# Set-up: third key group masked earlier, values 0 to 3 made in another bank; the ends of attention and the border reordered

## Chip, cores and metric

The kernel runs on one core of a Trainium2 chip. The metric is the device time in microseconds (us), the median of three runs. Engines are named as in the profile: PE (TensorE, matmul), DVE (VectorE), ACT (ScalarE), POOL (GpSimd), SP (the queue that issues plain DMAs). Each engine takes its instructions strictly in the order of the program and waits on semaphores.

## The reference, cut to what matters

There are 16 sequences of 128 tokens with 128 features (x), and a context of 77 rows of 64 features for each. Two layers run one after the other:

```
x = x + tanh(g_xattn[l]) * cross_attention(layernorm(x), ctx)   # 16 heads of 8, softmax over the 77 rows
x = x + tanh(g_ffn[l])   * moe(layernorm(x))                    # 8 experts of 128 -> 512 -> 128, top 2 per token
```

Layer 0's experts use the tanh form of GELU, without biases; its combination weights are the two top softmax probabilities, normalised to sum 1. Layer 1 has biases everywhere, ReLU experts, and its moe is `layer_norm(t + sum of the two experts) * gamma + beta`, with t the normalised x. All is float32.

## The kernel before

**Set-up.** Weights and context are turned on PE. Keys and values of layer 0 come from `keys` (PE), masked to a block form by `masked` (ACT or DVE), and `vals` (PE), masked by `values_kept` (DVE, counted by the semaphore `v_kept`). Group g of the keys holds six batches; group 2 lies in bank 7 of the eight PSUM banks. Values of batches 0 to 3 (`VE` = 4) are made at once in bank 2, batches 4 to 15 one at each step of attention (`late_batch`, `more_values`). `upper_scores` of batch 0 waits for `v_kept` to reach 4. `unread` issues n matmuls of 512 columns whose result nobody reads.

**Attention** is a software pipeline, written out by hand, of steps s = 0 to 17 (`B` = 16) and a `tail`, and each engine has its own `step(s)`. In step s, batch s is normalised and turned, batch s-1 gets its q, batch s-2 its scores (first pass: `scores_for_max`, from which DVE's `maxima` takes each head's maximum; second pass: `scores`, from which `less_max` subtracts it; then four Exp on ACT), and batch s-3 the weighted values, the division and `residual`. Banks 2 and 3 hold the upper first scores.

**Routing** works on pairs of batches, named by the odd one. `row_stats` (DVE), `deviations` (POOL), a normalisation into `xfa` (POOL; by DVE for the last pair), `turn_rows` (PE), `copied` (ACT), `logits` (PE), `read_logits` and `choose` (DVE: top two), `ranks` (PE: how many earlier tokens went to each expert), `counted` (POOL: running count), `read_ranks` and `place` (DVE: row numbers), `scatter` (POOL: an indirect DMA per batch and choice, into the row buffer `xg_rows`). `chosen(s)` and `placed(s)` say which pair is chosen and which is placed in step s: s-6 and s-7 where these are odd. The last pairs are LAST = 15, PRIOR = 13, THIRD = 11; THIRD is ranked and placed in the tail.

**Route.** When all is counted, `route` (DVE) computes for 39 tiles of 128 rows the expert `t_e`, the first row `r_row`, which rows are valid and where results go; `tiles0`/`tiles1` tell the others. `gate_gaps` and `gate_weights` make the two combination weights. SP (`load_tiles`) waits for the flag and for all scatters, then loads tiles into four buffers.

**Experts.** In step s of the tile loop PE turns tile s, does the first stage of tile s-1 and the second of tile s-2; ACT copies the turned tile and applies the activation; DVE copies the expert's w1 for tile s (`w1s`, two buffers), computes the destination rows `ids` of tile s-1 and copies the result of tile s-2 out; POOL scatters the result into `o_rows`. SP reloads a buffer when its `ids` are computed.

**Border.** After layer 0's loop PE makes the values of layer 1's batches 0 to 7, DVE runs `late` (biases and gains of layer 1) and masks these values, SP gathers the results, and DVE adds them to x (`stats_of`) and takes the statistics of layer 1's first batches.

## Time and profile before

| what | value |
|---|---|
| median of 3 runs | 464.51 us (464.02 to 465.03) |
| profiled execution: its own time | 464.98 us |
| its span | 463.2 us, 15660 instructions |
| PE matmul busy | 382.5 us, 83% |
| DVE busy | 328.4 us, 71% |
| POOL busy | 232.8 us, 50% |
| ACT busy | 214.1 us, 46% |
| attention, layer 0, with set-up | 0 to about 115 us |
| expert tiles, layer 0 | about 134 to 213 us |
| attention, layer 1 | about 227 to 327 us |
| expert tiles, layer 1 | about 346 to 424 us |

The rows further down come from this one profiled execution; their times count from the start of its span. A busy share is an average over stages with different limits, so it does not say by itself which engine sets a stage. TensorE's granted clock has two levels here, 1.2 and 2.4 GHz.

### The profile page before, as it was taken

The numbers are of one execution on the slowest core, as the hardware profiler recorded it, in microseconds if no ns is written. First come the engines' busy times: TensorE is split into PE (matmuls) and PEld (weight loads), VectorE is DVE, ScalarE is ACT, GpSimd is POOL, SyncE is SP. The second block draws the span as 40 slices with busy tenths as digits, with TensorE's granted clock in tenths as the row PEclk, the third lists the DMA queues.
The fourth block names the chain that finished last, engine by engine and source line by source line (L and its number), as shares of the span: only waits on it lengthen the run. The fifth ranks groups of instructions, "written<-read, shape, count | busy, mean of one in ns | idle before, by whom it ended". The sixth has DMA issues, their size and how long they took to land.

```text
span 463.2 us, 15660 instructions
## 1 busy us (share of the span) xinstructions
PE 382.5 (83%) x5357; PEld 306.1 (66%) x5357; DVE 328.4 (71%) x1164; ACT 214.1 (46%) x607; POOL 232.8 (50%) x370
## 2 busy tenths in 40 slices
PE   8699999997839999999899988998739999997000
PEld 4466666665539999996356666666729999997000
DVE  4558899987765666667558989987654666666592
ACT  3534555544514444441255555553525666665022
POOL 7313367768713544453203357767742445455176
PEclk9879999999559999998979999999888999999555
DMA  6969000011112222221201010001211223221612
GB/s 174 331 143 297 5 16 27 28 34 38 52 48 56 72 72 73 72 66 51 71 18 33 26 36 28 27 28 54 68 55 44 72 66 77 71 77 43 186 36 57
DMA packets 38690, 32.73 MB, mean 71 GB/s; under 512 B 6984, under 2 KB 32245, under 8 KB 38613
## 3 DMA queue, kind: packets, MB, share of 16 engines
q1 hardware_dynamic: 34069, 22.12, 18.0%
q0 software_dynamic: 4544, 9.61, 6.6%
q8 instruction: 45, 0.74, 0.7%
q14 instruction: 32, 0.26, 0.2%
HBM read 20.50 MB, written 11.21 MB: 68 GB/s over the span
## 4 chain that ended last, share of the span: by engine, by line
PE 57%; DVE 17%; issue 9%; POOL 9%; DMA 5%; ACT 1%; SPq 1%; DVEq 0%; POOLq 0%; ACTq 0%
PE banks L693 52%; PE banks L696 5%; DVE mx L1337 4%; POOL xg_rows L575 4%; DMA room<-xg_rows 2%; DVE room L1404 2%; DVE x L1321 1%; POOL wa L670 1%; DMA xg_rows<-xfa,slots 1%; DVE mxp L1346 1%; DVE wa L1635 1%; DMA o_rows<-room,ids 1%; DVE fstats L1422 1%; DVE wa L1628 1%; ACT room L1103 1%
## 5 line engine op out<-in xcount | busy, mean ns | idle before, releaser
L648 POOL DMA_INDIRECT o_rows<-room,ids x78 | 76.4, 980 | 96.4 <-DVE room L1572 44.6
L693 PE MATMUL banks<-room 128*128 128x128 f32 x624 | 86.0, 282 | 0.8 <-ACT room L1196 0.2
L693 PE MATMUL banks<-wa,room 128*128 x624 | 82.9, 276 | 0.5 <-ACT room L1191 0.4
L693 PEld LDWEIGHTS banks<-room 128*128 128x128 f32 x624 | 78.6, 198 | 2.7 <-issue 2.6
L693 PEld LDWEIGHTS banks<-wa,room 128*128 128x128 f32 x624 | 76.1, 192 | 0.9 <-issue 0.8
L575 POOL DMA_INDIRECT xg_rows<-xfa,slots x64 | 64.2, 1003 | 20.1 <-issue 18.8
L1103 ACT ACTIVATE room<-banks 128x384 f32<-128x384 f32 x128 | 52.4, 496 | 28.2 <-PE banks L693 28.2
L1337 DVE TENSOR_REDUCE mx<-banks 128x8 f32<-128x648 f32 x64 | 50.2, 825 | 12.2 <-PE banks L693 11.9
L1196 ACT ACTIVATE room<-banks,b_cols 128x128 f32<-128x128 f32 x156 | 44.6, 368 | 26.5 <-PE banks L693 26.1
L1058 ACT ACTIVATE room<-banks 128x128 f32<-128x128 f32 (+1 forms) x110 | 31.2, 283 | 49.0 <-PE banks L696 49.0
L1549 DVE COPY room<-wa 128x512 f32 x78 | 33.3, 427 | 28.7 <-issue 21.4
L1404 DVE RECIPROCAL room<-banks 128x128 f32<-128x128 f32 x32 | 30.5, 953 | 7.4 <-PE banks L693 7.2
L1191 ACT ACTIVATE room<-banks 128x512 f32<-128x512 f32 x39 | 23.3, 598 | 26.1 <-PE banks L693 26.1
L693 PE MATMUL banks<-kz,room 32*128 32x324 f32 x256 | 32.8, 499 | 3.0 <-issue 2.2
L696 PE MATMUL banks<-ident,room 128*128 128x128 f32 x78 | 22.5, 288 | 15.4 <-DMA room<-xg_rows 14.9
L693 PE MATMUL banks<-room,kz 32*128 32x128 f32 x768 | 32.8, 301 | 0.4 <-issue 0.4
L693 PE MATMUL banks<-room,keep 128*32 128x128 f32 x768 | 28.8, 285 | 2.3 <-ACT room L1103 2.3
L693 PEld LDWEIGHTS banks<-room,v_s 128*32 128x32 f32 x768 | 20.1, 113 | 15.1 <-ACT room L1103 14.6
L693 PE MATMUL banks<-room,v_s 128*32 128x128 f32 x768 | 28.8, 285 | 0.3 <-DVE x L1413 0.2
L693 PEld LDWEIGHTS banks<-room,kz 32*128 32x128 f32 x768 | 26.4, 198 | 2.8 <-issue 0.5
L565 POOL TENSOR_SCALAR rstd<-mv 128x2 f32<-128x2 f32 x16 | 3.8, 239 | 45.9 <-DVE mv L1307 42.1
L693 PE MATMUL banks<-wide 128*128 128x512 bf16 x85 | 24.7, 452 | 1.4 <-POOLq L286 1.4
(188 smaller groups left out, 656.3 us busy)
## 6 DMA issues: line engine op xcount, KB each, us to landing
room<-xg_rows SPq DMA_DIRECT2D x78, 68.5 KB, 1.9
wa<-in_L_ffn_w SPq DMA_DIRECT2D x1, 2048.0 KB, 10.4
wb<-in_L_ffn_W SPq DMA_DIRECT2D x1, 2048.0 KB, 16.7
ob<-o_rows SPq DMA_DIRECT2D x32, 64.0 KB, 2.0
wb<-o_rows SPq DMA_DIRECT2D x6, 256.0 KB, 4.8
o_rows<-room,ids POOLq DMA_INDIRECT x78
x<-in_x SPq DMA_DIRECT2D x4, 256.0 KB, 4.4
xg_rows<-xfa,slots POOLq DMA_INDIRECT x64
```

The source lines that it names most:

```text
L575: pool.indirect_dma_start(out=xg_dram, in_=xfa[:, at, :], in_offset=None, out_offset=bass.IndirectOffsetOnAxis(ap=slots[:, at, k:k + 1], a ...
L648: pool.indirect_dma_start(out=o_dram[l], in_=o_sb[t.slot(UN)][:, :], in_offset=None, out_offset=bass.IndirectOffsetOnAxis(ap=ids[t.slot(UN ...
L670: pool.tensor_tensor(nrm[:, b, :], nrm[:, b, :], gam[:, :], ALU.mult).then_inc(l_gam, 1)
L693: return pe.matmul(out_, lhsT, rhs, start=start, stop=stop)
L696: return pe.transpose(out_, in_, idn[0:n, 0:n])
L1058: return act.activation(out_, in_, ACT.Copy)
L1103: act.activation(probs[b.slot(2)][g][:, :], bank[(4, 5, 0, 1)[g]][0:M, 0:NC * T], ACT.Exp)\
L1191: act.activation(hid[:, :], bk[:, :], func).then_inc(S["act"].sem, FC)
L1196: act.activation(hid[:, c * P:(c + 1) * P], bk[:, c * P:(c + 1) * P], func, bias=b1_cols[:, bass.ds(e4 + c, 1)]).then_inc(S["act"].sem, 1)
L1337: dve.tensor_reduce(mx[r][:, G * g:G * (g + 2)].rearrange("p (i j) -> p i j", i=2), two.rearrange("p i (j k) -> p i j k", j=G), AX.X, ALU. ...
L1404: dve.reciprocal(den[:, :], bank[6][:, T:2 * T]).then_inc(rc.sem, 1)
L1549: dve.tensor_copy(w1s[s.slot(2)][:, :], wa1[:, bass.ds(e, F)]).then_inc(S["wc"].sem, 1)
```

## The change

- Set-up: DVE masks key group 2 (bank 7) in step 1 and no longer in step 2. `vals` of batches 0 to 3 go to bank 7 in step 2, behind the first scores of batch 0, and their masking follows batch 0's `maxima`. The first scores no longer wait for `v_kept`. Two filler matmuls of four go.
- Ends of attention, both layers: pair THIRD is chosen in step 16 and ranked and placed in step 17, not in the tail; POOL's scatters of pairs 7, 9 (FOURTH) and 11 are put in another order; pair PRIOR is normalised by DVE (`normalised`), not POOL.
- `route`: the tile rows come from sums of differences instead of a selection by expert, and a new flag `rowsT` is told as soon as they are there; SP's tile loads wait for it instead of `tiles`.
- Masked values of layer 1: batches 8 to 11 behind the route; batches 12 to 15 at steps 2 to 5 of layer 0's tile loop on DVE. `gate_weights` moves to step 6 of both loops, `late` to step 8 of layer 0's, the scaled weights `w01g` to its step 10.
- ACT runs a one-column Gelu ahead of layer 0's tiles and a one-column Exp behind them (`preload`).
- Filler matmuls: 34 and 18 instead of 12 behind the attention of layers 0 and 1; 30 instead of 42 at the border.

The diff, without the declarations of tiles and flags:

```diff
@@ -239,6 +238,9 @@
...
         altbase = sb("altbase", [P, NT])
+        region7 = sb("region7", [P, E])
+        first_row = sb("first_row", [P, NT])
+        preload = sb("preload", [P, 2])
@@ -369,12 +371,17 @@
...
         def chosen(s):
+            if s.c >= B:
+                return THIRD if s.c == B else None
...
         def placed(s):
+            if s.c > B:
+                return THIRD
...
-        LAST, PRIOR, THIRD = Step(B - 1), Step(B - 3), Step(B - 5)
+        LAST, PRIOR, THIRD, FOURTH = Step(B - 1), Step(B - 3), Step(B - 5), Step(B - 7)
@@ -445,7 +452,7 @@
...
                 S = layers[l]
-                hear(sp, f"tiles{l}")
+                hear(sp, f"rowsT{l}")
@@ -555,6 +562,9 @@
...
                 iota(altbase[:, :], [[P, NT]], NPAIR, 1)
+                iota(first_row[:, :], [[P, NT]], P, 0)
+                link(pool.memset(region7[:, :], float(REGION)))
+                link(pool.memset(region7[:, E - 1:E], 0.0))
@@ -599,10 +609,16 @@
...
                         deviations(b4)
+                    if live_pair(b4) and b4.c < B - 3:
...
                                                frs[:, j, 1:2], ALU.subtract, ALU.mult).then_inc(S["f2"].sem, 1)
+                    if s.c == B:
+                        placed_rows(FOURTH.back(2))
+                        scatter(FOURTH.back(2), 1)
+                    if s.c == B + 1:
+                        scatter(FOURTH, 1)
@@ -617,21 +633,22 @@
...
                         counted(placed(s))
-                    for b, js in ((b8, (0, 1) if s.c == B + 1 else (0,)), (b9, (1,))):
-                        if live_pair(b):
+                    for b, js in ((b8, (0,)), (b9, (1,))):
+                        if live_pair(b) and s.c < B:
...
                                 scatter(b, j)
+                    if s.c == B:
+                        placed_rows(FOURTH)
+                        scatter(FOURTH, 0)
+                    if s.c == B + 1:
+                        placed_rows(THIRD)
+                        scatter(THIRD, 0)
                 def tail():
-                    counted(THIRD)
-                    placed_rows(THIRD)
-                    scatter(THIRD, 0, (0,))
+                    scatter(THIRD, 1)
                     deviations(LAST)
-                    scatter(THIRD, 0, (1,))
-                    scatter(THIRD, 1, (0,))
                     counted(PRIOR)
-                    scatter(THIRD, 1, (1,))
@@ -716,7 +733,7 @@
...
-                return ("kza0_0", "kzd0_0") if (l, g) == (0, 0) else ("kzd0_2",) if (l, g) == (0, 2) else (f"kza{l}_{g}",)
+                return ("kza0_0", "kzd0_0") if (l, g) == (0, 0) else () if (l, g) == (0, 2) else (f"kza{l}_{g}",)
@@ -749,10 +766,7 @@
...
                     if s == 0:
-                        unread(bank[2][:, :], 4)
-                    if s == 1:
-                        for b in range(VE):
-                            vals(0, b, bank[2][:, b * NC * G * HD:])
+                        unread(bank[2][:, :], 2)
@@ -788,7 +802,6 @@
...
                         hear(pe, "woS")
-                        pe.wait_ge(v_kept, VE)
@@ -911,6 +922,10 @@
...
                         lower_scores(b2)
+                    if l == 0 and s.c == 2:
+                        hear(pe, "kzd0_2")
+                        for b in range(VE):
+                            vals(0, b, bank[7][:, b * NC * G * HD:])
@@ -921,6 +936,8 @@
...
                         ranks(placed(s), s)
+                    if s.c == B:
+                        logits(THIRD, bank[7])
@@ -930,7 +947,7 @@
...
                         project(b3)
-                    if live_pair(b5):
+                    if live_pair(b5) and s.c < B:
@@ -943,6 +960,8 @@
...
                             S["f3"].wait(pe, chosen(s), 1)
+                        if placed(s):
+                            S["f4"].wait(pe, placed(s), 1)
@@ -951,7 +970,6 @@
...
                     values(LAST, bank[5])
-                    ranks(THIRD, Step(B + 2))
@@ -1035,7 +1053,7 @@
...
                 tail()
-                unread(bank[2 if l == 0 else 4][:, :], 12)
+                unread(bank[2 if l == 0 else 4][:, :], 34 if l == 0 else 18)
@@ -1047,7 +1065,7 @@
...
                     S["oc"].wait(pe, Step(NT - 1))
-                    unread(bank[0][:, :], 42)
+                    unread(bank[0][:, :], 30)
@@ -1170,6 +1188,8 @@
...
                     say(act.activation(gexp[:, :], gap[:, :], ACT.Exp), f"gexp{l}")
+                    if l == 0:
+                        act.activation(preload[:, 0:1], zero_row[:, 0:1], ACT.Gelu_apprx_tanh)
@@ -1208,6 +1228,8 @@
...
                 pipeline(act, NT, 8, 1, experts(l))
+                if l == 0:
+                    act.activation(preload[:, 1:2], zero_row[:, 0:1], ACT.Exp)
@@ -1267,12 +1289,8 @@
...
                         hear(dve, "keep")
-                    if s == 2:
+                    if s == 1:
                         masked(2, range(G), bank[7])
-                    if s == 1:
-                        dve.wait_ge(v_made, VE)
-                        for b in range(VE):
-                            values_kept(b, bank[2][:, b * NC * G * HD:])
@@ -1431,6 +1449,8 @@
...
                         maxima(b2)
+                    if l == 0 and s.c == 2:
+                        kept_from(range(VE), bank[7], 0)
@@ -1438,6 +1458,10 @@
...
                         read_ranks(placed(s))
+                        if s.c > B:
+                            place(placed(s))
+                    if s.c == B + 1:
+                        normalised(PRIOR)
@@ -1453,24 +1477,26 @@
...
                         row_stats(b3)
-                    if placed(s):
+                    if placed(s) and s.c <= B:
...
+                def normalised(b):
+                    S["rs2"].wait(dve, b)
+                    for j in range(2):
+                        dve.tensor_scalar(xfa[:, b.c - 1 + j, 0:D], x[:, seq(b.back(1 - j))], fmv[:, j, 0:1],
+                                          frs[:, j, 1:2], ALU.subtract, ALU.mult).then_inc(S["f2"].sem, 1)
...
                     S["lg"].wait(dve, PRIOR)
-                    read_ranks(THIRD)
                     read_logits(PRIOR, bank[7])
-                    place(THIRD)
...
                     choose(PRIOR)
-                    S["rs2"].wait(dve, LAST)
-                    for j in range(2):
-                        dve.tensor_scalar(xfa[:, LAST.c - 1 + j, 0:D], x[:, seq(LAST.back(1 - j))], fmv[:, j, 0:1],
-                                          frs[:, j, 1:2], ALU.subtract, ALU.mult).then_inc(S["f2"].sem, 1)
+                    normalised(LAST)
@@ -1493,26 +1519,24 @@
...
                 total(cE[:, :], cmp8[:, :, :])
-                link(tt(fE[:, :], cE[:, :], tE[:, :], ALU.subtract))
+                link(dve.scalar_tensor_tensor(dA[:, :], tE[:, :], float(-P), region7[:, :], ALU.mult, ALU.add))
+                link(tt(dB[:, :], region7[:, :], nE[:, :], ALU.subtract))
+                link(tt(dB[:, 0:E - 1], dB[:, 0:E - 1], nE[:, 1:E], ALU.add))
                 link(tt(t8a[:, :, :], inner(iotat[:, :], E), bc3(cE[:, :], NT), ALU.is_ge))
+                link(tt(t8b[:, :, :], t8a[:, :, :], bc3(dA[:, :], NT), ALU.mult))
+                total(t_up[:, :], t8b[:, :, :])
+                link(tt(t8b[:, :, :], t8a[:, :, :], bc3(dB[:, :], NT), ALU.mult))
+                total(t_end[:, :], t8b[:, :, :])
+                link(tt(t_up[:, :], t_up[:, :], first_row[:, :], ALU.add))
+                link(dve.scalar_tensor_tensor(t_row[:, :], t_end[:, :], nE[:, 0:1], t_up[:, :], ALU.add, ALU.min))
+                link(dve.tensor_copy(r_row[:, :], t_row[:, :]))
+                tell(dve, f"rowsT{l}")
                 total(t_e[:, :], t8a[:, :, :])
-                link(tt(t8a[:, :, :], bc3(iota8[:, :], NT), inner(t_e[:, :], E), ALU.is_equal))
-                link(tt(t8b[:, :, :], t8a[:, :, :], bc3(nE[:, :], NT), ALU.mult))
-                total(t_n[:, :], t8b[:, :, :])
-                link(tt(t8b[:, :, :], t8a[:, :, :], bc3(fE[:, :], NT), ALU.mult))
-                total(t_f[:, :], t8b[:, :, :])
-                link(tt(t_j[:, :], iotat[:, :], t_f[:, :], ALU.subtract))
-                link(ts(t_j[:, :], t_j[:, :], float(P), None, ALU.mult))
-                link(ts(t_n[:, :], t_n[:, :], float(-P), None, ALU.add))
-                link(tt(t_rel[:, :], t_j[:, :], t_n[:, :], ALU.min))
                 link(ts(t_ec[:, :], t_e[:, :], float(E - 1), None, ALU.min))
-                link(dve.scalar_tensor_tensor(t_row[:, :], t_ec[:, :], float(REGION), t_rel[:, :], ALU.mult, ALU.add))
-                link(ts(r_row[:, :], t_row[:, :], float(P), None, ALU.add))
...
-                link(dve.scalar_tensor_tensor(t_valid[:, :], t_rel[:, :], iotap[:, :], t_j[:, :], ALU.add, ALU.is_ge))
+                link(dve.scalar_tensor_tensor(t_valid[:, :], t_row[:, :], iotap[:, :], t_up[:, :], ALU.add, ALU.is_ge))
@@ -1574,25 +1598,29 @@
...
                         ins.then_inc(S["oc"].sem, 1)
+                    if l == 0 and 2 <= s.c < 6:
+                        kept_from((s.c + 10,), bank[7][:, (s.c - 2) * NC * G * HD:], B + 4 + s.c - 2)
+                    if s.c == 6:
+                        gate_weights(l)
+                    if l == 0 and s.c == 8:
+                        dve.wait_ge(ld["w1"], 16 * len(LATE))
+                        late()
+                    if l == 0 and s.c == 10:
+                        link(dve.tensor_scalar(w01g[:, :], w01[:, :], tg[:, 2:3], None, ALU.mult))
...
                 link(dve.memset(cum[:, :], 0.0))
-                if l == 1:
-                    link(dve.tensor_scalar(w01g[:, :], w01[:, :], tg[:, 2:3], None, ALU.mult))
...
                 tail()
-                if l == 0:
-                    kept_from(range(8, 12), bank[5], B)
...
                 if l == 0:
-                    kept_from(range(12, B), bank[7], B + 4)
-                gate_weights(l)
+                    kept_from(range(8, 12), bank[5], B)
@@ -1600,8 +1628,6 @@
...
                 if l == 0:
-                    dve.wait_ge(ld["w1"], 16 * len(LATE))
-                    late()
...
                 else:
```

## Rows read from the trace of the kernel before

**Rows 1.** The page, clock in 40 slices; chain that ended last, by engine.

```profile
PEclk9879999999559999998979999999888999999555
...
PE 57%; DVE 17%; issue 9%; POOL 9%; DMA 5%; ACT 1%; SPq 1%; DVEq 0%; POOLq 0%; ACTq 0%
```

**Rows 2.** Timeline of set-up: start, length, engine, line, tile [idle before, its end].

```profile
13.85 3.13 ACT L1066 ACTIVATE kz<-banks,zero_row,mask 128x486 f32<-128x486 f32 x4
...
14.71 1.95 DVE L1243 TENSOR_TENSOR v_s<-banks,keep_v 128x384 f32<-128x384 f32 x4 [2.79 <-PE banks L693]
...
16.88 0.83 PE L693 MATMUL banks<-kz,room 32*128 32x324 f32 x8 [2.23 <-issue]
...
17.74 1.57 DVE L1337 TENSOR_REDUCE mx<-banks 128x8 f32<-128x648 f32 x2 [1.07 <-PE banks L693]
...
20.00 1.67 PE L693 MATMUL banks<-room,kz 32*128 32x128 f32 x24
...
20.16 2.29 DVE L1238 TENSOR_SCALAR kz<-banks,mask 128x324 f32<-128x324 f32 x4
```

**Rows 3.** Timeline of the end of attention, layer 0.

```profile
112.97 0.20 DVE L1367 MAX8 top<-lg 128x8 f32<-128x8 f32 x2
...
113.85 0.18 DVE L1379 TENSOR_TENSOR mb<-oh 128x16 bf16<-128x16 f32 x1
...
115.35 0.60 DVE L1472 TENSOR_SCALAR xfa<-x,fmv,frs 128x128 f32<-128x128 f32 x2 [1.32 <-POOL frs L567]
...
119.86 0.96 POOL L575 DMA_INDIRECT xg_rows<-xfa,slots  x1 [0.30 <-issue]
```

**Rows 4.** Timeline of the route, layer 0: a wide step, the tile rows.

```profile
125.19 0.48 DVE L1500 TENSOR_TENSOR room<-iota,t_e 128x312 f32<-128x312 f32 x1
...
129.34 0.33 DVE L1512 TENSOR_SCALAR r_row<-t_row 128x39 int32<-128x39 f32 x1
```

**Rows 5.** Timeline of the first tiles, layer 0.

```profile
133.99 0.45 PE L696 MATMUL banks<-ident,room 128*128 128x128 f32 x1 [7.57 <-DMA room<-xg_rows]
...
137.53 1.28 ACT L1191 ACT_TABLE_LOAD   x1 [1.86 <-PE banks L693]
...
139.55 1.15 PE L693 MATMUL banks<-wa,room 128*128 x8 [0.40 <-ACT room L1191]
```

**Rows 6.** Timeline of a steady tile, layer 0.

```profile
143.23 0.43 DVE L1549 COPY room<-wa 128x512 f32 x1 [0.30 <-issue]
...
144.44 1.06 PE L693 MATMUL banks<-room 128*128 128x128 f32 x8
144.53 0.29 DVE L1572 COPY room<-banks 128x128 f32<-128x128 f32 x1 [0.25 <-PE banks L693]
...
145.12 0.43 DVE L1549 COPY room<-wa 128x512 f32 x1 [0.29 <-issue]
```

**Rows 7.** Timeline of the border between the layers.

```profile
213.33 0.20 DVE L1287 CAST bo<-bo_in 1x128 bf16<-1x128 f32 x1
...
216.62 10.92 PE L693 MATMUL banks<-wide 128*128 128x512 bf16 x42
216.65 3.81 DVE L1243 TENSOR_TENSOR v_s<-banks,keep_v 128x384 f32<-128x384 f32 x8
...
220.80 0.74 DVE L1321 SCALAR_TENSOR_TENSOR x<-ob,w01g,x 128x128 f32<-128x128 f32 x2
...
225.65 0.49 ACT L1111 ACTIVATE xn<-x,rstd 128x128 f32<-128x128 f32 x1 [13.85 <-POOL rstd L617]
...
227.38 0.27 PE L696 MATMUL banks<-ident,xn 128*128 128x128 f32 x1
...
232.46 1.28 ACT L1103 ACT_TABLE_LOAD   x1
```

**Rows 8.** Timeline of the first tiles, layer 1.

```profile
346.18 0.45 PE L696 MATMUL banks<-ident,room 128*128 128x128 f32 x1 [6.51 <-DMA room<-xg_rows]
...
350.95 1.17 PE L693 MATMUL banks<-wa,room 128*128 x8
```

More of the change, by code:

```diff
@@ L191, in build @@
         cE = sb("cE", [P, E])
-        fE = sb("fE", [P, E])
+        dA = sb("dA", [P, E])
+        dB = sb("dB", [P, E])
         t8a = part("experts", P, NT * E).rearrange("p (t e) -> p t e", t=NT)
@@ L195, in build @@
         t_e = sb("t_e", [P, NT])
-        t_n = sb("t_n", [P, NT])
-        t_f = sb("t_f", [P, NT])
-        t_j = sb("t_j", [P, NT])
-        t_rel = sb("t_rel", [P, NT])
+        t_up = sb("t_up", [P, NT])
+        t_end = sb("t_end", [P, NT])
         t_valid = sb("t_valid", [P, NT])
@@ L281, in build @@
                     f"{k}{l}_{g}" for l in range(2) for k, n in (("k", 3), ("kzd", 3), ("kza", 3))
-                    for g in range(n)) + tuple(f"{k}{l}" for l in range(2) for k in ("count", "tiles", "gap", "gexp"))}
+                    for g in range(n)) + tuple(f"{k}{l}" for l in range(2) for k in ("count", "rowsT", "tiles", "gap", "gexp"))}
         def tell(eng, name):
@@ L849, in more_values @@
                     if late_batch(s.c) is not None:
-                        if late_batch(s.c) == VE:
-                            hear(pe, "kzd0_2")
                         pe.wait_ge(v_kept, late_batch(s.c))
```

## The prediction

> **What bounds it now.** I read the page first. The chain that ended last is 57% TensorE and 17% VectorE [rows 1], and no engine sets the whole: attention alternates between PE and DVE, the expert tiles are paced by PE, and at four seams (set-up, the end of each attention, the border between the layers) PE waits for others. The clock line shows the same seams: full speed is 9, and slices 1 and 2 (from 11.6 to 34.7 us), 10 and 11 (115.8 to 139.0), and some around the border and the start of layer 1's tiles are lower [rows 1]. Then I read the timeline at each seam.
>
> In set-up the first scores start at 16.88, after PE idled 2.23 us; just before, DVE finished the masked values of batches 0 to 3 at 14.71 + 1.95 = 16.66, the count that the scores wait for [rows 2]. At the end of attention POOL issues scatters at 0.96 + 0.30 = 1.26 us each; eight (pairs 13 and 15) run without a gap from 119.86, so the last ends at 119.86 + 7 x 1.26 + 0.96 = 129.64 [rows 3], and the first tile reaches PE at 133.99, awaited by DMA [rows 5]. A steady tile takes 145.12 - 143.23 = 1.89 us, and DVE idles only 0.25 in it [rows 6]. At the border layer 1's first transpose, at 227.38, stands behind 42 filler matmuls that take 10.92 us; its input was ready at 225.65 + 0.49 = 226.14 [rows 7].
>
> **1. Set-up.** Removed: the wait for the values ahead of the first scores. Q is scaled on ACT just before ACT starts its masking at 13.85 [rows 2], so the scores can start near 14.0, not 16.88. DVE's masking of key group 2 (2.29 us [rows 2]) moves into the gap of 2.79 us ahead of the values [rows 2]: from about 11.95 to 14.25. It hides behind the wait for the first scores; were it later than 14.85, maxima would be late by the difference. First maxima: scores 14.0 + 0.86 (17.74 - 16.88) = about 14.85, against 17.74: 2.9 earlier. What is late next is ACT: the second score pass also needs batch 1's q, which ACT gives only behind its masking, at 13.85 + 3.13 = 16.98 [rows 2], so that pass starts near 17.6 and not 20.00, 2.4 earlier. The values' 1.95 us of DVE now follow the first maxima, and end near 18.8 (14.85 + 1.57 + 0.4 for two small ones + 1.95), before the second scores exist near 20. POOL's iota and two memsets add under 1 us to a queue whose next result, the third batch's statistics, is not late. The second price is the clock: two slices at 8 and 7 tenths [rows 1] mean 11.58 x (0.4 + 0.6) = 11.6 us at half speed. If it stays as it is, I take 3.0; if PE, with fewer gaps, kept 2.4 GHz, half of the 5.8 us that PE-bound work would lose comes back as well, to 5.9. I take 4.0, nearer the first end, because PE still has holes while it waits for maxima and q.
>
> **2. Ends of attention, both layers.** Pair 11 is now chosen, ranked and placed a step sooner, and pair 7's second scatter goes ahead of POOL's wait for ranks: both fill idle POOL time. Against it, in step 16 PE's logits (about 0.5) stand before the transpose of the maxima, and DVE's choice (112.97 to 114.03, 1.06 [rows 3]) before batch 15's maxima: the last batch is 1.5 us later. POOL no longer normalises pair 13, but its deviations of pair 15 now stand behind both scatters of pair 11 and one more half of pair 9. Counted from place(9) at about 104.6 in that order (six scatters at 1.26 through pair 11, two deviations at 1.1, count 0.5, issue gaps of 0.3 to 0.5), they end at 117.8, against 115.35 [rows 3]; DVE waits in order for them, then places pair 13 at 118.95, and pair 13's scatters start at 119.25, not 119.86: **-0.6 per layer** (bounds -1.5, if all POOL idle closed, and +0.9). Queued behind DVE's wait are pair 13's slots and pair 15's logits; pair 15's placing comes 2.45 later.
>
> The route: its tile rows ended at 129.34 + 0.33 = 129.67. Values 8 to 11 (1.95 by rows 2) leave the stretch before it; two wide steps of 0.51 (0.48 and a gap) and a few small ones go, 1.6 together; place(15) adds 2.45. So the new flag comes at 129.67 - 1.95 - 1.6 + 2.45 = 128.6, ahead of the scatters' landing: the sooner flag is worth nothing here, and the cover is about 2 us [rows 3, 4].
>
> **3. First tiles.** In layer 0 PE went from the first transpose (133.99) to the first second-stage matmul (139.55) in 5.56 us, at half clock and with a table load of 1.28 [rows 1, 5]. 34 fillers instead of 12 start near 124.8: some 7 at 0.43 and 27 at 0.21 (slow and fast form of the same matmul: 10.92/42 = 0.26 is their mix [rows 7]) end near 133.5, when the first tile arrives at 133.4. At full clock the transpose halves, the two first-stage groups take about 1.0 each (1.06 in rows 6) and the table is there: 3.2 us. So 5.56 - 3.2 + 0.6 = **-2.9** (only -1.0 if the clock is down; fillers that run over cost up to +1). In layer 1: 350.95 - 346.18 = 4.77 [rows 8] becomes 3.4 if six more fillers hold the clock: with the 0.6, **-2.0** (clock down: -0.6).
>
> The row gives the load 1.28, with the Gelu ready to follow at its end [rows 5]. The Trainium skill (ScalarE: Activation LUTs, "What ACT_TABLE_LOAD costs") adds a drain of about 1.38 us, 2.66 for a switch; by it the border below would win 1.4 more and the sum would be 9.8 instead of 8.4. The row decides against it.
>
> **4. DVE work moved into layer 0's loop.** Four value batches at steps 2 to 5 (1.95/4 = 0.49, single 0.55: 2.2), the gate weights at step 6 (three small ones, 0.75 with their gaps), the late biases at step 8 (213.33 to 216.65, 3.3 [rows 7]): 6.2 us, where DVE idles 0.25 a tile and the copy of w1 is ready at 143.66 for a matmul at about 144.35, 0.7 of slack [rows 6]. Over steps 2 to 8: 6.2 - 7 x 0.25 - 0.7 = 3.8 of PE standing still, 2.7 of it after step 8. PE is the pace, so it is lost: **+3.8** (bounds 0, if the work fits gaps that the start leaves, and 6.2). The loads of later tiles wait for DVE's ids, 3.3 later too, but PE is late by nearly as much. The scaled weights at step 10 are one small instruction, inside a tile's 0.25. In layer 1 the gate weights alone meet 0.7 + 0.25 of slack: 0 to 0.1.
>
> **5. Border.** DVE's queue ahead of the first combination at 220.80 loses the 3.3, but waits for the values (v 0 to 3 near 214.4, 4 to 7 near 216.7) and the gathered rows, which land near 219.3: 1.5 sooner. That makes the first normalised batch ready at 226.14 - 1.5 = 224.6. Twelve fillers fewer (0.21 to 0.26 each) free PE at 227.38 - 2.55 = 224.8. So the transpose is **-2.5** (bounds 1.5 and 3.1). The Exp table's 1.28 at 232.46 [rows 7] stood behind a wait that ends 0.45 later: **-0.8** (to -1.28).
>
> **Sum.** -4.0 - 2.9 + 3.8 - 2.5 - 0.8 - 2.0 = -8.4. The profiled execution took 464.98 (span 463.2 and 1.78 around it): 456.6; the runs' median is 0.47 below it: **456.1 us**, 1.8% faster. 0.2%, 0.9 us, is about what a measurement of this kernel tells from no change.
>
> **Rivals.**
> - *Half clock.* Fillers and holes don't hold 2.4 GHz: set-up -3.0, layer 0's tiles -1.0, layer 1's -0.6, the rest the same: -3.0 - 1.0 + 3.8 - 3.3 - 0.6 = -4.1, 460.4. For it: the clock was low at every one of these seams [rows 1]. Against: the fillers now reach to the first tile. 0.18.
> - *DVE's pieces are hidden in the loop* (the first tiles leave it slack): -12.2, 452.3. Against: 0.25 idle a tile [rows 6]. 0.10.
> - *The order at the end of attention costs.* DVE waits for POOL's deviations behind scatters; if the last scatters end 1.9 later and not 0.6 sooner, twice: -8.4 + 5.0 = -3.4, 461.1. For it: DVE already sat 1.32 for them [rows 3]. Against: the eight scatters were the bound, and DVE's wait must pass 2 us to displace them. 0.10.
> - *Slower: PE's clock falls after the standstill at step 8.* At 1.2 GHz a tile is PE-bound at 3.8, so each tile loses 1.9; it decides from (8.4 + 0.9)/1.9 = 4.9 tiles, some 19 us at half clock. For ten tiles: -8.4 + 19 = 475. For it: a tile's transpose and w1 copy resume after 2.7 us of silence. Against: the dips at the seams are one or two slices long [rows 1]. 0.05.
> - *It does nothing:* the seams close, but each gain is paid back at the next wait, as with the 3.8. Within 0.9 of 464.5. 0.05.
>
> **Chances and range.** My forecast, with the clock of set-up either way (454.2 to 457.6), has 0.52; the rivals share the other 0.48. From 452 to 461.3 it leaves out the slower case, no change, and tails: 0.15 to 0.2. Faster by over 0.2%: 0.90; within 0.05; slower 0.05.
>
> **What would show it.** First maxima near 14.9 and second near 20.2; slices 1 and 2 of the clock line; first scatter of pair 13 near 119.3 on its own count, less the set-up's gain; first tile to second-stage matmul 3.2 us with no table load; PE's idle before the first-stage matmuls of tile 9 about 2.7 us, waiting for the w1 copy; first transpose of layer 1 2.5 us nearer to the last tile. Wrong if the late biases stall nothing, if the fillers run past the first tile, or if the scatters' end moves later.

## The result, and the profile after

The changed kernel took 461.0 us, median of five runs (459.81 to 462.1), the kernel before 464.44 beside it: ratio 0.9936, 95% interval 0.9915 to 0.9956. It is 3.4 us faster; 8.4 were forecast. The profiled execution took 461.97, its span is 460.1, 3.1 less than before, and that is where the stages below are read.

The page, clock in 40 slices, which answers to [rows 1]:

```profile
PEclk9589999999599899999769999999899999999555
```

Slice 1 is now at 5 tenths and the border (slices 19 and 20) at 7 and 6, where before it was 9 and 9. Timelines of the changed kernel (start, length, engine, line, tile, idle before and what ended it); set-up, against [rows 2]:

```profile
13.88 1.46 PE L710 MATMUL banks<-kz,room 32*128 32x324 f32 x8
...
15.40 1.57 DVE L1355 TENSOR_REDUCE mx<-banks 128x8 f32<-128x648 f32 x2 [1.47 <-PE banks L710]
```

The scores start at 13.88, as forecast, but run at half clock (1.46, not 0.83), so first maxima came at 15.40, not 14.9. Batch 14's maxima moved from 98.74 to 95.69: 3.05. (In the three quiet profiles with the old set-up they come at 97.60 to 98.74, in the six with the new one at 93.86 to 95.87, so the means are 3.1 apart; "quiet" is explained below.)

End of attention and first tiles, against [rows 3 to 5]:

```profile
115.84 1.06 POOL L585 DMA_INDIRECT xg_rows<-xfa,slots  x1 [1.00 <-DVE slots L1415]
...
121.48 9.08 PE L710 MATMUL banks<-wide 128*128 128x512 bf16 x33 [0.33 <-issue]
...
124.95 0.18 DVE L1533 CAST r_row<-t_row 128x39 int32<-128x39 f32 x1
...
130.40 0.27 PE L713 MATMUL banks<-ident,room 128*128 128x128 f32 x1
...
133.59 1.15 PE L710 MATMUL banks<-wa,room 128*128 x8
```

From batch 14's maxima to the first tile it takes 34.71 instead of 35.25, and from there to the first second-stage matmul 3.19 instead of 5.56: 2.9 in all, as forecast. Step 8 of layer 0's loop, where `late` stands, against [rows 6]:

```profile
146.79 0.20 DVE L1305 CAST bo<-bo_in 1x128 bf16<-1x128 f32 x1
...
150.52 0.43 DVE L1573 COPY room<-wa 128x512 f32 x1 [0.70 <-DVE bet L1317]
...
151.09 1.13 PE L710 MATMUL banks<-room 128*128 128x128 f32 x8 [2.01 <-DVE room L1573]
...
152.06 1.59 PE L710 MATMUL banks<-wa,room 128*128 x8
```

PE stands still for 2.01 us, waiting for w1's copy, and then its matmuls take 1.59 where they took 1.06: the granted clock is at 0.50 for 3.4 us, from 152.4. In stretches:

```profile
146.00:150.00 4.00, 2.77 (x23) 2.38 (x22) 3.39 (x15) 1.48 (x4) 1.93 (x2) 1.00 0.27 72
150.00:154.00 4.00, 2.91 (x19) 2.94 (x20) 2.56 (x11) 0.70 (x2) 0.96 (x1) 0.80 0.07 20
154.00:158.00 4.00, 4.00 (x30) 4.00 (x29) 2.09 (x9) 1.32 (x4) 1.21 (x2) 0.77 0.26 68
```

(Stretch; then its length, busy us of PE, weight loads, DVE, ACT and POOL with their counts; then the granted clock, the DMA share and GB/s.) The border, against [rows 7]:

```profile
213.76 6.42 PE L710 MATMUL banks<-wide 128*128 128x512 bf16 x29 [0.16 <-issue]
223.41 0.33 PE L713 MATMUL banks<-ident,xn 128*128 128x128 f32 x1 [3.23 <-ACT xn L1129]
...
225.36 1.46 PE L710 MATMUL banks<-kz,room 32*128 32x324 f32 x8 [0.24 <-ACT room L1148]
```

```profile
218.02 0.74 DVE L1339 SCALAR_TENSOR_TENSOR x<-ob,w01g,x 128x128 f32<-128x128 f32 x2 [1.71 <-DMA ob<-o_rows]
```

In the kernel before PE had 10.92 us of fillers here and came late; now they end at 220.2, PE idles 3.23, and the scores run at half clock. DVE idles 1.71 for the gathered rows. The first tiles of layer 1, against [rows 8]:

```profile
342.77 0.30 PE L713 MATMUL banks<-ident,room 128*128 128x128 f32 x1 [2.30 <-DMA room<-xg_rows]
343.61 0.45 PE L713 MATMUL banks<-ident,room 128*128 128x128 f32 x1 [0.54 <-ACT room L1076]
344.10 2.05 PE L710 MATMUL banks<-room 128*128 128x128 f32 x8
```

The fillers end 2.30 before the tile, and the first group takes 2.05, half clock again.

In some sets of runs the kernel before took 463 to 466 us (below: quiet), in others 493 to 496, where PE idled in attention with nothing to wait for (below: starved; the last section shows it), and there the ratios say little of the edits but the stages outside attention can still be read.

### The profile page after: what moved, and what is told of

The parts are those of the page before. It is cut to its first block, busy times and chain, and to the rows that moved or that the text cites. A ratio compares the mean times of both kernels' runs of the same rounds, so it can differ in the third digit from the quotient of the medians.

```text
span 460.1 us, 15686 instructions
## 1 busy us (share of the span) xinstructions
PE 387.5 (84%) x5368; PEld 308.5 (67%) x5371; DVE 326.1 (71%) x1164; ACT 214.7 (47%) x609; POOL 229.6 (50%) x369
## 4 chain that ended last, share of the span: by engine, by line
PE 50%; DVE 17%; POOL 14%; issue 11%; DMA 5%; ACT 1%; DVEq 0%; ACTq 0%; SPq 0%; POOLq 0%
PE banks L710 46%; POOL xg_rows L585 7%; PE banks L713 4%; DVE mx L1355 4%; DMA o_rows<-room,ids 3%; DVE room L1422 2%; DVE x L1339 2%; POOL wa L687 1%; POOL frs L577 1%; DVE mxp L1364 1%; DVE stats L1322 1%; DVE wa L1661 1%; DVE wa L1654 1%; POOL xfa L615 1%; DVE lst L1664 1%
## 5 line engine op out<-in xcount | busy, mean ns | idle before, releaser
L710 PE MATMUL banks<-kz,room 32*128 32x324 f32 x256 | 34.7, 525 | 0.4 <-ACT room L1148 0.2
L710 PE MATMUL banks<-wide 128*128 128x512 bf16 x96 | 25.9, 429 | 2.0 <-POOLq L288 1.4
```

Of the source, the lines that this page charges most:

```text
L710: return pe.matmul(out_, lhsT, rhs, start=start, stop=stop)
```

## The experiments

Stages are differences between two events of one profile, so they don't hold what happened ahead of them: *loop* is first second-stage matmul to last result copy of layer 0, *border* the last copy to layer 1's first maxima, *start* layer 1's first to third batch's maxima, *tile 1* first transpose to first second-stage matmul.

**42 fillers at the border** (quiet)

```diff
-                    unread(bank[0][:, :], 30)
+                    unread(bank[0][:, :], 42)
```

> The changed kernel (461.0 us) with 42 filler matmuls at the border again instead of 30. Theory 1, the clock: 30 fillers at full clock end at 220.2 and PE stands still for 3.2 us before layer 1's first transpose at 223.41, and the granted clock falls at 223.5. Twelve more at 0.21 fill 2.5 of the 3.2; the clock stays at 2.4 GHz through 226, the first transpose stays near 223.4, first maxima of layer 1 come 1.0 sooner (2.5 behind the transpose as before the change, not 3.5), and the following steps gain 0.5 to 1.5 more: 1.5 to 2.5 us in all, 458.5 to 459.5. Theory 2, the gathered rows bound the border and the clock falls anyway because PE has holes there: the first transpose and the first maxima stay where they are, 460.8 to 461.2. A third outcome: the fillers run over the transpose, 461.5.

459.84, ratio 0.9873 (0.9837 to 0.9908). Beside the version of layer 1's fillers below, which is the same up to layer 1's tiles, the border took 15.14 instead of 16.03 and the stretch to batch 14's maxima 80.84 instead of 81.49: 1.5 won, at the low end of theory 1. From the last copy to batch 14's maxima it takes 96.0 and 95.8 in the two quiet profiles with 42 fillers and `late` off the border, 97.4 and 97.5 in the two with 30. The scores of the first batch took 0.83; but the clock fell all the same, at 228.15, which is 6.7 us behind the first transpose and not 0.7, and stayed down for 6.8 us and not 13.7:

```profile
220.00:224.00 4.00, 3.76 (x24) 1.82 (x22) 0.58 (x4) 1.68 (x5) 1.31 (x5) 1.00 0.29 83
224.00:228.00 4.00, 2.31 (x36) 1.38 (x35) 2.92 (x8) 1.77 (x5) 0.17 (x1) 1.00 0.06 17
228.00:232.00 4.00, 4.00 (x40) 2.25 (x42) 2.01 (x4) 1.23 (x5) 0.00 (x0) 0.52 0.06 16
```

(Columns as above.) PE is busy 2.31 of 4 us ahead of the fall: it waits 1.69 for the first maxima.

**`late` behind the loop again** (quiet)

```diff
-                    if l == 0 and s.c == 8:
-                        dve.wait_ge(ld["w1"], 16 * len(LATE))
-                        late()
...
+                    dve.wait_ge(ld["w1"], 16 * len(LATE))
+                    late()
                     kept_from(range(4), bank[3], B + 8)
```

> The changed kernel with the late biases and gains (late) back behind layer 0's tile loop on DVE, where they were, and all else kept. Theory A, the loop pays for late twice, in PE's wait of 2.0 for the w1 copy and in a clock that falls behind it: the last result copy of layer 0, at 211.00, comes 4.4 sooner (2.7 stall, 1.7 clock) near 206.6, and at the border late takes DVE for 3.3 while the gathered rows land, of which 1.7 was idle anyway, so 0.5 to 1.5 comes back: 457 to 458. Theory B, the prediction's own sum: only the 2.7 of the stall comes back, and the border loses 1.6 to 3.3: 460 to 461.5. If the clock still falls near 150 without late, it is the value batches or the early tiles that make it fall.

455.87, ratio 0.9787 (0.9752 to 0.9823): the lowest ratio of all. The loop took 74.38, beside 77.56 with `late` in it in the same set of runs: 3.2 back. At `late`'s own place more came back: from the seventh to the eleventh result copy it takes 7.98 here, 11.99 to 12.00 in all five profiles with `late` in step 8, and 7.6 to 7.9 in the five others that have the rest of the work in the loop and not `late` in step 8. So `late` cost 4.0 to 4.4, theory A; the clock fell behind it in all five (3.4 us at 0.50, 1.7 us of work) and in none of the six. The rest of the difference lies in single tiles that come 0.3 to 0.6 late, others in each profile. The border paid 0.5 (16.53 for 16.03). These stages explain some 3 us; the ratio lies 7 us under the changed kernel's 0.9936, which was not run again in this set, so the ratio is not all this edit's.

The value batches were still in steps 2 to 5, and cost nothing: the first five result copies are 7.7 us apart in this version and the changed one, 8.0 before. DVE took them between a result copy and w1's next copy without a gap:

```profile
137.75 0.29 DVE L1596 COPY room<-banks 128x128 f32<-128x128 f32 x1 [0.18 <-PE banks L710]
137.96 0.55 DVE L1265 TENSOR_TENSOR v_s<-banks,keep_v 128x384 f32<-128x384 f32 x1
138.42 0.42 DVE L1573 COPY room<-wa 128x512 f32 x1
```

In [rows 6] that copy has 0.30 of idle ahead of it, put down to issue. With a piece before it that idle is gone, so DVE's room in a tile was 0.25 + 0.30, not 0.25. The gate weights at step 6 did cost: the next two result copies take 4.1 us and not 3.8, in every version with them there.

**28 fillers behind layer 1's attention** (quiet)

```diff
-                unread(bank[2 if l == 0 else 4][:, :], 34 if l == 0 else 18)
+                unread(bank[2 if l == 0 else 4][:, :], 34 if l == 0 else 28)
```

> The changed kernel with 28 instead of 18 filler matmuls behind layer 1's attention. PE idled 2.3 us between the last filler (340.47) and the first tile (342.77), and the clock fell at 343.8. Theory 1, the clock: ten more at 0.21 take 2.1 and close that hole; the first tile's transpose stays near 342.8, and the first second-stage matmul follows in 3.4 instead of 4.67: 1.3 sooner, 459.7. Theory 2, holes between the tile's first steps let the clock fall whatever stands ahead of them: no change, 461.0. If the fillers run over the first tile: up to 0.5 slower.

459.73, ratio 0.9839 (0.9799 to 0.9879). Tile 1 took 3.61 instead of 4.67, and PE idled 0.41 ahead of it, not 2.30: 1.1 won, theory 1 (in the two other quiet versions with 18 fillers it took 4.53 and 5.23, in the other with 28 it took 3.58). The rest of the ratio is not this edit's.

**The set-up alone, on the kernel before** (quiet): the hunks of steps 0 to 2, `kept` and the wait for `v_kept`.

> The kernel before with only the change of the set-up: key group 2 masked in step 1, values 0 to 3 in bank 7 behind the first scores, two fillers of four. If the set-up gives its gain by itself: first maxima near 15.4 instead of 17.74, batch 14's maxima 3.0 sooner, 464.4 - 3.0 = 461.4, and the clock falls near 12 as in the changed kernel; then all other parts together (of which the prediction wanted -4.4) are worth only about -0.4. If part of these 3.0 comes from the new order in the last steps: 1.5 to 2.5 less than before, 462 to 463.

461.31, ratio 0.9915 (0.9878 to 0.9951), as much as the whole change. So all the other parts together gave about nothing in the changed kernel, within the some 2 us that the intervals leave; the table of stages below says the same.

**Four more fillers in set-up**, behind `woT` (starved; set-up lies ahead of where that bites)

```diff
                 say(tr(bank[3][:, 0:P], w_nat[:, 1, :], P), "woT")
+                unread(bank[1][:, :], 4)
```

> The changed kernel with four more fillers in set-up, where PE waited 1.2 us (10.82 to 12.03) for the first normalised batch. Theory 1, the clock of set-up falls for want of work there: with the hole closed it stays at 2.4 GHz to 28 us and batch 14's maxima come 1.0 to 1.5 sooner: 460 to 460.5. Theory 2: it falls by chance or for the holes behind (runs of the same set-up showed it fall at 12, at 19, or not at all): no change, 461.0.

502.34, ratio 1.0179 (1.0118 to 1.0241). They closed the hole (0.17 of idle instead of 1.21 ahead of the first transpose), and the clock fell at 17.9; in seven profiles with the new set-up and without these fillers it fell at 17.1 to 18.2:

```profile
16.00:20.00 4.00, 2.72 (x32) 1.88 (x34) 2.67 (x9) 2.54 (x8) 0.48 (x2) 0.74 1.06 298
20.00:24.00 4.00, 4.00 (x42) 2.32 (x44) 1.92 (x4) 1.23 (x6) 0.00 (x0) 0.50 0.94 252
```

Its fourth batch's maxima came at 33.2, as with `late` behind the loop (33.16). In three of the eleven other profiles of the changed set-up, all without these fillers, the clock did not fall in the first 40 us; in one of them, that of the 42 fillers at the border, those maxima came at 30.7 and batch 14's at 93.86, 4.9 sooner than before the change. So theory 1, the hole, fell, by this one profile. What decides between the two stays open; it is 1 to 2 us from one execution to the next. The Trainium skill (TensorE: Matmul & The Clock Gate, "Part 1: The HAM clock gate") says that the number of matmuls at the low clock at a kernel's start varies from run to run. What varies here is another thing, a fall from 12 us on, after the clock was up; no run here shows the start itself vary.

**The order at the ends of attention alone**, on the kernel before: all hunks of `chosen`, `placed`, steps 16 and 17 and the tails.

> The kernel before with only the new order at the ends of both attentions (pair 11 chosen, ranked and placed sooner, pair 13 normalised by DVE, POOL's scatters in the new order). The prediction gave it -0.6 per layer. From batch 14's maxima to the first tile the kernel before took 35.25 and 34.89, the changed one 34.71 and 34.41, so 0.5 per layer: 464.4 - 1.0 = 463.4. Rival: batch 15's later maxima (1.3 us) cost as much as POOL gains, and the 0.5 came from the route's sooner flag or from chance: 35.2 and 34.9 again, 464.2 to 464.8.

Starved: 502.12, ratio 1.0183 (1.0129 to 1.0236); repeated, still starved, 502.02, 1.0156 (1.0107 to 1.0204). Once more, quiet:

> The same kernel as e10_order_only. Where the kernel before takes 464: 463.4 if the new order is worth 0.5 per layer, 464.2 to 464.8 if batch 15's later maxima eat it. Where PE is short of instructions: 1.015 to 1.02, as twice before.

464.14, ratio 1.0035 (1.0009 to 1.006): no gain, rather a loss. The last scatter ended 23.75 behind the last maxima instead of 25.64 (of which 1.3 is only that the last maxima are later), but the first tile came 6.06 behind it instead of 4.31. The old flag, told behind `t_alt`, was the last; the scatters had ended at 127.94:

```profile
131.01 0.20 DVE L1538 TENSOR_TENSOR t_alt<-altbase,t_alt 128x39 f32<-128x39 f32 x1
```

```profile
132.04 2.82 SPq L466 DMA_DIRECT2D room<-xg_rows  x4
```

SP left 0.83 behind the end of this instruction. In the kernel before SP left 1.35 behind it, and 2.32 behind the end of the last scatter:

```profile
128.72 0.96 POOL L575 DMA_INDIRECT xg_rows<-xfa,slots  x1 [0.30 <-issue]
130.45 0.20 DVE L1517 TENSOR_TENSOR t_alt<-altbase,t_alt 128x39 f32<-128x39 f32 x1
132.00 7.53 SPq L461 DMA_DIRECT2D room<-xg_rows  x6
```

So the old flag had only some 0.5 us to spare there. So the order was tried together with the route's new arithmetic and flag:

> The kernel before with the new order at the ends of attention and with the route's new arithmetic and its sooner flag for the tile loads, nothing else. With the order alone the last scatter ended 23.7 behind the last maxima instead of 25.6, but the first tile came 6.06 behind it instead of 4.3, for the old flag was told at 131.2 and the load left at 132.0. Theory A, the flag is what the order needs: the first tile comes 4.3 behind the last scatter and 28.0 behind the last maxima (order alone 29.8, before 29.95), and the time is 1 to 2 us under the order alone, ratio 0.996 to 1.000. Theory B, the prediction's, that the sooner flag is worth nothing: as the order alone, 1.0035. For layer 1 the order alone already had 4.43 behind the scatter, so nothing changes there by either.

Starved: 500.32, ratio 1.0172 (1.0132 to 1.0212). But the first tile came 5.19 behind the last scatter, where the order alone in starved runs had 7.27 and 7.29: the flag, with the arithmetic that makes it sooner, is worth 2.1 there, theory A in kind, though not down to its 4.3. In a quiet run this pair was not measured.

**First tiles of layer 0 alone**, on the kernel before: 34 fillers and the one-column Gelu.

> The kernel before with only two edits at the first tiles of layer 0: 34 fillers instead of 12 and the one-column Gelu ahead of the tiles. The prediction's 5.56 to 3.2: first transpose to first second-stage matmul takes 3.2, 464.4 - 2.4 = 462.0. Rival: the sooner start is given back in the loop, where the first tiles then wait for DVE: 464. A second look at the same edit: without DVE's pieces in the loop, the stretch from first second-stage matmul to last copy should stay at 73.6 as in the kernel before, not 77.4.

Starved: 498.05, ratio 1.0062 (1.0022 to 1.0102); repeated, 495.76, 1.0043 (1.0009 to 1.0078). Tile 1 took 3.19 both times and the loop 73.59 and 73.27: nothing is given back in it. But the fillers ran over the tile, which came 10.0 behind the last scatter. The Gelu without more fillers, quiet:

```diff
+                    if l == 0:
+                        act.activation(preload[:, 0:1], zero_row[:, 0:1], ACT.Gelu_apprx_tanh)
```

> The kernel before with the one-column Gelu ahead of layer 0's tiles, and its 12 fillers kept. It splits the 5.56 to 3.19 between first transpose and first second-stage matmul: the table load took 1.28, so 4.3 if that is all that it costs, and the clock's share is 1.1; by the Trainium skill (ScalarE: Activation LUTs, what a table load costs) up to 2.66 would go with the load, and then 2.9 to 3.2 remain and the fillers are worth next to nothing here. In time: 463.2 or 462.1 where the kernel before takes 464.4. Where PE is short of instructions, the first tile comes 7 behind the last scatter and not 10, since 12 fillers don't reach it.

463.16, ratio 1.001 (0.9989 to 1.0031). Tile 1 took 5.22, only 0.34 less than 5.56, with the load moved ahead of the tile:

```profile
130.07 1.28 ACT L1175 ACT_TABLE_LOAD   x1
```

```profile
134.25 2.05 PE L694 MATMUL banks<-room 128*128 128x128 f32 x8
136.09 0.42 PE L697 MATMUL banks<-ident,room 128*128 128x128 f32 x1
136.30 1.92 PE L694 MATMUL banks<-room 128*128 128x128 f32 x8
138.01 1.83 PE L694 MATMUL banks<-wa,room 128*128 x8
```

The load ran beside PE's second group of the first stage, which at half clock ends at 138.2 anyway. The other 2.0 of the 2.4 came with the fillers, that is with the clock. This split holds in this order only: 34 fillers without the Gelu were not run, and at full clock the load would stick out by more.

**All three remedies**: 42 fillers, 28 fillers, and `late`'s eleven instructions one by one in steps 12, 14, ... 32.

```diff
-                    if l == 0 and s.c == 8:
-                        dve.wait_ge(ld["w1"], 16 * len(LATE))
-                        late()
+                    if l == 0 and 12 <= s.c < 34 and s.c % 2 == 0:
+                        late_piece((s.c - 12) // 2)
```

> The changed kernel with three edits: late's eleven small instructions one at a time in every second step of layer 0's tile loop from step 12, not all in step 8; 42 fillers at the border; 28 behind layer 1's attention. Theory 1: each piece of some 0.2 fits into DVE's 0.25 idle and the slack of w1's copy, so the loop (first second-stage matmul to last result copy, 77.4 in the changed kernel, 74.4 with late behind the loop) takes 74.4, the border keeps the changed kernel's short DVE queue (15.1 from last copy to first maxima), and layer 1's first tile takes 3.6: 461.0 - 3.0 - 1.4 - 1.2 = 455.4 on the changed kernel's count, 2% under the kernel before. Theory 2, DVE has no room in the loop at all and each piece is paid in full: the loop takes 76.5 or more, 457.5.

Starved, 506.02, ratio 1.0243 (1.0189 to 1.0297); repeated, 502.77, 1.0172 (1.012 to 1.0224). Then quiet:

> The same kernel as e9_best. In the last two sessions the kernel before took 493.5 to 493.9 and PE ran short of instructions in attention (idle before it without any wait, steps of 6.4 instead of 5.6 us); the border, the loops and layer 1's first tiles did there what theory 1 said. In a session where the kernel before takes 464 to 466, theory 1: 455.4, ratio 0.981. Theory 2, gains of one place are lost at the next: ratio 0.985 to 0.988. If the session is again one where PE is short of instructions: ratio 1.015 to 1.025, as twice before.

456.62, ratio 0.9883 (0.9837 to 0.9929). Loop 74.16 (74.68 and 74.16 starved), border 15.16, tile 1 3.58: every stage did what theory 1 said, and the profile's span is 452.9, 7.2 under the changed kernel's. The times don't bear it out: the ratio is the one that theory 2 gave (0.985 to 0.988), the interval touches the changed kernel's (0.9915 to 0.9956), and the six runs lie between 454.61 and 461.31, the profiled one being the fastest. Against `late` alone (0.9787, in another set) nothing more is shown to be won.

**The same with the old order at the ends of attention** (starved)

> e9_best with the kernel before's order at the ends of both attentions (steps 16 and 17 and the tail on PE, DVE and POOL), all else kept. If the new order is worth 0.5 per layer, this takes 1.0 more than e9_best: 456.4. If it is worth nothing, 455.4; if it costs, as the 1.3 by which batch 15's maxima came later may, it takes 454.5 and is the best version.

496.88, ratio 1.0045 (1.0001 to 1.0089), where the version above had 1.0172 beside it. Starved, the new order costs some 6 us. The profiles place 3.3 of it: in each layer batch 14's maxima come 8.0 to 8.8 us behind batch 13's with the new order and 6.4 to 6.7 with the old, in every starved profile, where quiet it is 5.2 with both. In the version above DVE idles 2.69 us there ahead of `residual`, here 1.39, and the profile names no engine of the core that ended the longer wait. The rest was not placed.

**The changed kernel again** (starved)

> The changed kernel itself, unedited, beside two others and the kernel before on one chip: its ratio was 0.9936 alone. If PE is not short of instructions: 0.990 to 0.996. It gives the measure for the two others, since the kernel before differs by 2 us from one set of runs to the next.

501.68, ratio 1.0132 (1.0081 to 1.0184): there the change makes the kernel slower.

**Seven fillers where PE waits for layer 1's first maxima**, on top of all three remedies (starved; the start of layer 1 lies ahead of where that bites)

```diff
+                    if l == 1 and s.c == 2:
+                        unread(bank[7][:, :], 7)
                     if live(b2):
                         turn_max(b2)
```

> e13_best with seven more fillers in layer 1's step 2, where PE waits 1.7 us for the first maxima. In every run so far the granted clock fell to 0.5 for some 8 us within the first 12 us of layer 1, with fillers ahead of it (at 226 to 232) or without (from 223). Theory 1, the hole behind the first maxima brings it down: with it filled the clock stays at 2.4 GHz, first to second batch's maxima take 5.2 to 5.5 instead of 6.4 to 8, and the whole is 1 to 2 us under e13_best: ratio 0.984. Theory 2, it comes down somewhere in this stretch whatever PE does: same as e13_best, 0.988. If the fillers delay the transpose of the maxima: 0.2 to 0.5 us back.

504.62, ratio 1.0136 (1.0061 to 1.0212). The clock stayed up here, alone of the twenty profiles of this case; in the other nineteen it fell to 0.50 within the first 12 us of layer 1:

```profile
244.00:248.00 4.00, 3.71 (x23) 1.93 (x23) 0.93 (x2) 1.73 (x6) 1.38 (x4) 1.00 0.20 57
248.00:252.00 4.00, 3.82 (x43) 1.82 (x41) 2.62 (x8) 2.07 (x7) 0.00 (x0) 1.00 0.11 33
```

The same stretch without the seven, in the starved profile of all three remedies (layer 1's first maxima at 243.06 there, 247.07 here):

```profile
244.00:248.00 4.00, 2.90 (x36) 2.06 (x38) 2.07 (x7) 2.07 (x7) 0.00 (x0) 0.79 0.11 33
248.00:252.00 4.00, 4.00 (x56) 2.49 (x50) 1.92 (x4) 0.96 (x4) 0.00 (x0) 0.50 0.00 0
```

The start took 10.33 us, against 12.54, 12.62 and 12.84 in the three profiles of all three remedies, 13.48 in the changed kernel (12.54 starved) and 13.24 before: 2.2 won, theory 1. It is one profile, and what it gives in a quiet run was not measured.

## Why the prediction was right in direction and wrong in size

It forecast -8.4; its own terms, read as stages of the two profiles, came out so:

| term | forecast | measured |
|---|---|---|
| set-up | -4.0 | -3.05 |
| end of attention and tile 1, layer 0 | -2.9 | -0.54 - 2.37 = -2.9 |
| DVE's work in the loop | +3.8 | +3.84 |
| border, table | -2.5 - 0.8 | -0.8 |
| end of attention and tile 1, layer 1 | -2.0 | -0.5 - 0.1 = -0.6 |
| layer 1's tiles to the end | 0 | +0.4 |
| sum | -8.4 | -3.1 |

**The step that failed is 5, the border.** "Twelve fillers fewer free PE at 224.8" puts PE 11.7 behind the last copy; it was free 9.2 behind it, at 220.2. The 10.92 that the step scaled down were a mix with the half clock; now the fillers took 0.22 each at full clock. So the first transpose waited for its input, at 223.41: 14.26 behind the last copy became 12.41, 1.85 won for the 2.5 forecast, since the first combination came 7.02 behind the last copy, 0.66 sooner than before and not 1.5. What the step left out is the clock, which its price of fewer fillers put at nothing: behind 3.23 us of idle the scores and what followed ran at 1.2 GHz, for 13.7 us in all, so 1.0 was lost by the first maxima, and the table load's 0.8 did not show (start 13.48, before 13.24). Border and table gave 0.8 instead of 3.3, nearly half of the whole miss. Both fillers experiments bear it out: twelve more gave 1.5, and seven more in the next hole 2.2 (one starved profile). Theory 2 of the first of them, that the gathered rows alone set the border and fillers change nothing, fell.

**The next is layer 1's tile 1**, in step 3: "if six more fillers hold the clock" was the right condition with the wrong answer. Six did not reach (2.30 idle); sixteen did, and gave 1.1 of the 1.4 forecast. This half of the rival "half clock" came true, at layer 1 and in set-up, not at layer 0's first tile; its 460.4 was the forecast that came nearest for a reason that the runs show. The rival of the order gives 461.1, but by chance: its condition was false, for the scatters ended 0.7 and 0.3 sooner in the two layers, counted from batch 14's maxima, and not 1.9 later.

**Set-up, step 1.** The mechanism held (scores at 13.88, forecast 14.0), and its first end, 3.0, was the one to take: the clock did not stay up but fell sooner, at 12.5. The second maxima, at 21.81, missed the sign "near 20.2"; the step's own 2.4 off the 23.85 of before would have given 21.45. Alone, the set-up gave the whole of the measured gain.

**The loop, step 4, was right by luck.** The sum spread 6.2 over seven tiles and put the clock at nothing; in fact the values cost nothing, as DVE had 0.55 of room in a tile and not 0.25, the gate weights cost 0.3, and `late` cost 4.0 alone: 2.0 standing still, and 1.7 for the clock behind it, the small form of the rival "clock falls after the standstill", which lasted 3.4 us and not ten tiles. That is 4.3 where the loop as a whole shows 3.84, because the kernel before's profile had more late tiles elsewhere than the changed one's: its loop takes 72.7 to 73.6 in the nine profiles without the work, 73.57 in the one of the table.

**Step 2.** Forecast -0.6 per layer, measured -0.54 and -0.48 from batch 14's maxima to the tile. The new flag came where the step put it, ahead of the scatters' end (125.13 and 125.96). But "the sooner flag is worth nothing here" was false: with the new order and the old flag the tile came no sooner (6.06 behind the last scatter), and that version was not faster than before. The old flag had only 0.5 to spare, and the very edit that stands beside it used that up: the order ends the scatters 0.6 sooner in that version, counted from batch 14's maxima, and places the last pair later, so the old flag comes 1.7 later.

**Step 3, layer 0.** 3.2 forecast, 3.19 measured, but taking away the table load alone gave 0.34 of the 2.37, and the fillers with their clock gave 2.0. The row's 1.28 was already too much as a price, since only what sticks out behind PE's slow matmuls is on the path. The 2.66 for a switch of the Trainium skill (ScalarE: Activation LUTs, "What ACT_TABLE_LOAD costs"), quoted in that step, would have made it more still; the trace doesn't bear it out. The fillers ran over the tile a little: it came 2.30 behind SP's load, 1.96 to 1.99 in three quiet profiles with 12, so some 0.3 of the 0.6 was given back.

**The range in the last lines** is off by a slip: with the set-up at either of its ends the sum gives 454.2 to 457.1, not 457.6.

## What to carry to other kernels

Count fillers by the clock that they themselves bring about: at full clock they take half as long (0.21 and 0.43 from one to the next here), and a batch sized at half clock ends before the hole does. Where a helper engine makes PE wait, add what the clock loses behind the wait: here 1.7 us behind 2.0. Price a block of work on a helper engine by its longest stretch against the slack of the next consumer, not by its sum, and cut it in pieces before moving it, or leave it where it is: here the pieces and the old place took the same time in the loop (74.16 and 74.38). Value two edits at one seam together: whichever stops being last, the other becomes it.

## What the hardware showed that was not expected

The same program took 463 to 466 us in some sets of runs and 493 to 496 in others, once on the same chip. Starved, PE idles with nothing to wait for. End of layer 0's attention in the profile of all three remedies, starved:

```profile
136.49 0.35 PE L710 MATMUL banks<-wv,ctxT 65*32 65x32 f32 x4 [0.40 <-issue]
137.24 0.35 PE L710 MATMUL banks<-wv,ctxT 65*32 65x32 f32 x5 [0.41 <-issue]
...
141.69 8.38 PE L710 MATMUL banks<-wide 128*128 128x512 bf16 x33 [0.33 <-issue]
149.91 0.27 PE L713 MATMUL banks<-ident,room 128*128 128x128 f32 x1
```

and the same code, quiet:

```profile
118.78 1.11 PE L710 MATMUL banks<-wv,ctxT 65*32 65x32 f32 x64
119.83 9.03 PE L710 MATMUL banks<-wide 128*128 128x512 bf16 x34
128.91 0.30 PE L713 MATMUL banks<-ident,room 128*128 128x128 f32 x1
```

Four or five matmuls go each 0.75 us, where 64 took 1.11. Such idle sums to 17.1 us in this starved profile and to 1.8 in the quiet one of the same kernel; PE is also busy for 405.5 us and not 386.6, with the same matmuls, for more of them run at half clock. A step of attention takes 5.6 us up to the eighth batch, as ever, and 6.4 to 8 after it; the tile loops are untouched (77.41 quiet and 77.36 starved for the changed kernel). PE reaches the fillers so late that 34 of them delay the first tile: it comes 10 behind the last scatter, 7.3 with 12. That PE's instructions arrive late is an inference from the idle time, and what delays them is open: the two instruction queues on the page moved 45 and 32 packets, 0.74 and 0.26 MB, in both conditions. A version tuned by what its fillers fill is tuned for one of these conditions: the change is 0.6% faster in one and 1.3% slower in the other.
